# Softmax row sums in a two-head attention loop: matmuls over every probability tile against pair sums made on VectorE

## The reference, cut to what matters

```
x  : 8192 tokens x 4096, 32 heads, no mask, no causal cut
xn = layernorm(x)
q  = (xn @ Wq_c.T + bq_c) @ Wq_up.T + bq_up        # 192 per head: 128 + 64 rope
kv = xn @ Wkv_c.T + bkv_c                          # 512 latent + 64 rope, shared by the heads
k  = [kv_nope @ Wkv_up.T (128 per head), kv_rope]  ; v = 128 per head
attn = softmax(q @ k.T / sqrt(192))
out  = sum over heads of (attn @ v) @ Wo.T + bo    ; x = x + out
x    = x + layernorm(x) @ W.T + bias + LoRA terms
```

## Time and profile before

| | |
|---|---|
| runs before | 10136.65 and 9846.27 us, median 9991.46 us |
| the profiled execution | 9699.19 us |
| its span on the slowest core (core 5) | 9697.6 us |
| spans of the eight cores | 9638.9 to 9697.6 us |
| mean granted TensorE clock of core 5 | 0.839 |

### The profile page before, as it was taken

One profiled execution on the slowest core, in us unless ns is written; L12 is line 12 of the kernel. 1 busy time (PEld: TensorE's weight loads), 2 busy tenths in 40 slices (PEclk: granted clock), 3 DMA queues, 4 the chain that ended last, 5 costly groups with the idle time before them and its releaser, 6 DMA issues.

```text
span 9697.6 us, 97205 instructions; the slowest of 8 cores (9638.9 to 9697.6 us)
## 1 busy us (share of the span) xinstructions
PE 7616.9 (79%) x31944; PEld 2593.5 (27%) x31944; DVE 2710.9 (28%) x4102; ACT 3183.7 (33%) x5467; POOL 112.3 (1%) x232
## 2 busy tenths in 40 slices
PE   5464666666669889889899898898898898894777
PEld 2121323322222232332331331331322322311333
DVE  2012343344430330330331321321322312305211
ACT  1001222222205336336335345344354353351000
POOL 0100000000000000000000000000000000000000
PEclk8666666666679999999999999999999999995788
DMA  3634121121130000000000000000000000004444
GB/s 80 117 63 108 55 75 70 71 74 58 63 82 1 21 21 1 21 14 7 21 14 8 21 7 14 21 1 21 21 1 21 21 1 21 7 1 124 89 108 110
DMA packets 86382, 400.15 MB, mean 41 GB/s; under 512 B 9763, under 2 KB 22180, under 8 KB 67236
## 3 DMA queue, kind: packets, MB, share of 16 engines
q1 hardware_dynamic: 57574, 274.92, 8.1%
q0 software_dynamic: 28352, 119.03, 7.4%
HBM read 466.78 MB, written 46.14 MB: 53 GB/s over the span
## 4 chain that ended last, share of the span: by engine, by line
PE 73%; DVE 10%; issue 7%; DMA 7%; ACT 1%; DVEq 0%; SPq 0%; ACTq 0%; POOL 0%; POOLq 0%
PE ps L647 7%; PE ps L617 7%; PE ps L623 7%; PE ps L653 7%; PE ps L304 6%; PE ps L339 6%; PE ps L501 5%; PE ps L931 5%; PE ps L650 5%; PE ps L656 5%; PE ps L523 5%; PE ps L620 4%; DMA arena<-wqcT 3%; PE ps L548 3%; DVE st_sum L232 3%
## 5 line engine op out<-in xcount | busy, mean ns | idle before, releaser
L632 ACT ACTIVATE arena<-ps,sb_negc_col 128x512 bf16<-128x512 f32 x2048 | 1412.0, 689 | 3240.1 <-DVE sb_negc_col L605 1734.9
L634 ACT ACTIVATE arena<-ps,sb_negc_col 128x512 bf16<-128x512 f32 x2048 | 1397.0, 682 | 0.0
L304 PE MATMUL ps<-sb_id,arena 128*128 128x128 f32 x2048 | 775.8, 434 | 781.6 <-DVE arena L261 556.1
L666 DVE RECIPROCAL sb_recip<-ps 1x512 f32<-1x512 f32 x64 | 209.8, 3314 | 3956.3 <-PE ps L656 3956.3
L647 PE MATMUL ps<-arena 128*128 128x512 bf16 x2048 | 809.1, 395 | 35.2 <-DVE arena L691 35.2
L617 PE MATMUL ps<-arena 128*128 128x512 bf16 x2048 | 813.2, 397 | 27.8 <-ACT arena L634 27.8
L627 PE MATMUL ps<-arena 64*128 64x512 bf16 x2048 | 808.6, 395 | 0.0
L623 PE MATMUL ps<-arena 64*128 64x512 bf16 x2048 | 808.5, 395 | 0.0
L620 PE MATMUL ps<-arena 128*128 128x512 bf16 x2048 | 796.0, 389 | 0.0
L650 PE MATMUL ps<-arena 128*128 128x512 bf16 x2048 | 786.0, 384 | 0.0
L656 PE MATMUL ps<-arena,sb_onec 128*1 128x512 bf16 x2048 | 781.4, 382 | 0.0
(11 more groups left out here) (91 smaller groups left out, 5690.4 us busy)
## 6 DMA issues: line engine op xcount, KB each, us to landing
arena<-x_rot SPq DMA_DIRECT2D x72, 2048.0 KB, 10.0
arena<-wqcT POOLq DMA_DIRECT2D x128, 384.0 KB, 4.8
arena<-qcF_dram SPq DMA_DIRECT2D x32, 1536.0 KB, 6.4
arena<-wffn_til POOLq DMA_DIRECT2D x16, 2048.0 KB, 24.0
arena<-wqup_til POOLq DMA_DIRECT2D x16, 1152.0 KB, 11.8
x_dram<-arena SPq DMA_DIRECT2D x64, 256.0 KB, 4.1
arena<-x_dram SPq DMA_DIRECT2D x8, 2048.0 KB, 31.1
out_c<-arena SPq DMA_DIRECT2D x64, 256.0 KB, 2.4
```

Of the source, the lines that this page charges most:

```text
L304: tok_tp = em("t", lambda t, b=b, xb=a_xn[bi], dc=dc: t.transpose(bank(b)[:, 0:128], xb[:, dc * 128:dc * 128 + 128], sb_id[:, :]), sm_t)
L632: te0 = em("s", lambda s, b0=b0, kc=kc: s.activation(b_P[0][kc % 3], bank(b0), AF.Exp, bias=sb_negc_col[:, :]), sm_s)
L634: te1 = em("s", lambda s, b1=b1, kc=kc: s.activation(b_P[1][kc % 3], bank(b1), AF.Exp, bias=sb_negc_col[:, :]), sm_s)
```

## The change

The ones-matmuls no longer run on every probability tile. At each odd `kc`, VectorE adds the tile of step `kc - 1` and that of step `kc`, for each head (`tensor_tensor`, 128x512 bf16, all in SBUF), into a new tile `b_Ps[h][j]`, two per head, used in turn. `emit_pv` of an odd `kc` then runs the two ones-matmuls on the sums. `emit_pv` of an even `kc` has none. To make room, `b_bcast` and `b_otmp` go from two buffers each to one. New waits: an exp waits for the add that last read its tile (`p_read`), the ones-matmul for its add (`tps_tok`). The first PV matmul of a query block waits for banks 4 and 5 alone, the first ones-matmul for 6 and 7.

```diff
+        b_Ps = [[B.take(512, BF16) for _ in range(2)] for _ in range(2)]
...
                 wt("s", tok_sc)
+                wt("s", p_read[0][kc % 3])
+                wt("s", p_read[1][kc % 3])
                 te0 = em("s", lambda s, b0=b0, kc=kc: s.activation(
...
+                if kc % 2 == 1:
+                    for h, te in ((0, te0), (1, te1)):
+                        wt("v", te)
+                        wt("v", tps_free[h][(kc // 2) % 2])
+                        tok_add = em("v", lambda v, h=h, kc=kc: v.tensor_tensor(
+                            b_Ps[h][(kc // 2) % 2], b_P[h][(kc - 1) % 3],
+                            b_P[h][kc % 3], ALU.add), sm_v)
+                        tps_tok[h][(kc // 2) % 2] = tok_add
+                        p_read[h][(kc - 1) % 3] = tok_add
+                        p_read[h][kc % 3] = tok_add
...
-                em("t", lambda t, kc=kc: t.matmul(
-                    bank(6)[0:1, :], sb_onec[:, :], b_P[0][kc % 3],
-                    start=(kc == 0), stop=(kc == 63)))
-                return em("t", lambda t, kc=kc: t.matmul(
-                    bank(7)[0:1, :], sb_onec[:, :], b_P[1][kc % 3],
                     start=(kc == 0), stop=(kc == 63)),
                     sm_t if kc == 63 else None)
+                if kc % 2 == 1:
+                    j = (kc // 2) % 2
+                    if kc == 1:
+                        for ob in (6, 7):
+                            wt("t", bankfree[ob])
+                    for h in range(2):
+                        wt("t", tps_tok[h][j])
+                        tok = em("t", lambda t, kc=kc, h=h, j=j: t.matmul(
+                            bank(6 + h)[0:1, :], sb_onec[:, :], b_Ps[h][j],
+                            start=(kc == 1), stop=(kc == 63)),
+                            sm_t if kc == 63 else None)
+                        tps_free[h][j] = tok if kc == 63 else None
+                return tok
```

More of the change, by code:

```diff
@@ L431, in build_nc @@
         b_wkV = B.take(4 * 256, BF16).rearrange("p (c f) -> p c f", c=4)
-        b_bcast = [B.take(512, F32) for _ in range(2)]
-        b_otmp = [B.take(512, F32) for _ in range(2)]
+        b_bcast = B.take(512, F32)
+        b_otmp = B.take(512, F32)
+        b_Ps = [[B.take(512, BF16) for _ in range(2)] for _ in range(2)]
         b_osum = arena[:, OS_BASE:OS_BASE + 1024]
@@ L464, in build_nc @@
         texp = [(None, None)] * 3
+        tps_tok = [[None, None], [None, None]]
+        tps_free = [[None, None], [None, None]]
+        p_read = [[None] * 3, [None] * 3]
         tok_bc_prev = [None, None]
@@ L642, in emit_pv @@
                 if epi_banks_wait:
-                    for ob in (4, 5, 6, 7):
+                    for ob in (4, 5):
                         wt("t", bankfree[ob])
@@ L649, in emit_pv @@
                     start=(kc == 0), stop=(kc == 63)))
-                em("t", lambda t, kc=kc: t.matmul(
+                tok = em("t", lambda t, kc=kc: t.matmul(
                     bank(5), b_V[:, kc * 256 + 128:kc * 256 + 256], b_P[1][kc % 3],
-                    start=(kc == 0), stop=(kc == 63)))
-                em("t", lambda t, kc=kc: t.matmul(
-                    bank(6)[0:1, :], sb_onec[:, :], b_P[0][kc % 3],
-                    start=(kc == 0), stop=(kc == 63)))
-                return em("t", lambda t, kc=kc: t.matmul(
-                    bank(7)[0:1, :], sb_onec[:, :], b_P[1][kc % 3],
                     start=(kc == 0), stop=(kc == 63)),
                     sm_t if kc == 63 else None)
+                if kc % 2 == 1:
[11 more added lines that the diff above has]
+                return tok
             def emit_epi_v1(qb, tok_pv):
@@ L686, in flush_epi @@
                     wt("v", tok_bc)
-                    tcp = em("v", lambda v, bcb=bcb, h=h: v.tensor_copy(
-                        b_bcast[h], bank(bcb)), sm_v)
+                    tcp = em("v", lambda v, bcb=bcb: v.tensor_copy(
+                        b_bcast, bank(bcb)), sm_v)
                     bankfree[bcb] = tcp
@@ L691, in flush_epi @@
                     tmu = em("v", lambda v, h=h: v.tensor_tensor(
-                        b_otmp[h], bank(4 + h), b_bcast[h], ALU.mult), sm_v)
+                        b_otmp, bank(4 + h), b_bcast, ALU.mult), sm_v)
                     bankfree[4 + h] = tmu
@@ L695, in flush_epi @@
                     wt("v", tok_osum_chain[0])
-                    tok_osum_chain[0] = em("v", lambda v, qb=qb, h=h: v.tensor_tensor(
+                    tok_osum_chain[0] = em("v", lambda v, qb=qb: v.tensor_tensor(
                         b_osum[:, qb * 512:qb * 512 + 512],
-                        b_osum[:, qb * 512:qb * 512 + 512], b_otmp[h], ALU.add), sm_v)
+                        b_osum[:, qb * 512:qb * 512 + 512], b_otmp, ALU.add), sm_v)
             flush_fn[0] = flush_epi
```

## The result

The changed kernel takes 9445.01 us (median of 11 runs) against 10135.99 (median of 10) for the kernel before. In many executions the cores of a die are granted a lower clock for some of the time, whatever the kernel; the ratio leaves these out, and the profile of the changed kernel is read on the cores without it, 0 to 3. The ratio is 0.930, with a 95% interval of 0.920 to 0.939: faster, by 7%. It rests on few executions: the lowest were 9728 and 9788 us before, 9042, 9086 and 9093 us now. The sum had given a ratio of 0.948, 507 us less than the profiled execution.

A forecast was written before the change was run, and what follows sets the result against it. TensorE was taken to bound the kernel. 9699 - 532 + 3 + 22 gave 9192 us on the profiled execution, ratio 0.948, or 9469 on the median; the forecast was the middle, 9330, range 9130 to 9570.

The forecast's parts named there:

- The sum: Whole kernel: 9699 - 532 + 3 + 22 = 9192 us, 0.948 of the profiled execution.
- What bounds the kernel: Attention: TensorE sets the pace, busy throughout dense parts at clock 1.00, and ScalarE's exps wait for it.
- The signs: Profile after: right if double steps take 3.3 us; wrong if exps idle behind adds or the clock falls in dense stretches.
- Term 1: Attention steps: 1024 ones pairs removed at 0.52 us each, 532 us off TensorE.
- Term 2: Attention steps: 2048 VectorE adds hidden beside TensorE, except about 0.1 us at each of 32 block ends, 3 us.
- Term 3: Flush in the second query block: two adds ahead of the copy delay TensorE 1.4 us in 16 pairs, 22 us.
- Broken loads: Remaining ones pairs: a wait between the two matmuls stops the early weight load, 102 us more; chance 0.13.
- Loop over the tiles: Attention steps: exps, adds and next exps form a loop; at 1.0 us per add it costs 154 us; chance 0.04.
- Clock: Attention steps: denser full matmuls lower the clock; 1.2 GHz in 30% of double steps costs 774 us; chance 0.05.
- The estimate of 4.09: Attention double step in us, if a peak-current limit of 13/16 of the clock came with the change: 3.32 / 0.8125.

The follow-up runs named there:

- e4: The changed kernel without its adds and their waits, ones-matmuls reading only the odd step's tile: 3.213 us a double step, attention 5182 to 5185 us against 5196.
- e3: The kernel before plus the adds, the exps' waits for them and single flush buffers, sums never read: 3.840 us a double step, as in the kernel before.
- e1: The kernel before with 128 columns of ones as weights instead of one: 3.447 us a double step, 9311.5 us against 9706.9 for the run.
- e2: The kernel before with PV and ones-matmuls in turn instead of in pairs: 4.236 us a double step, spans 10217.7 to 10390.2 us.
- e5: The kernel before with 128 columns of ones and rope matmuls over all 128 rows: 3.453 us a double step, spans 9220.4 to 9287.9 us.
- e6: The changed kernel with 128 columns of ones as weights instead of one: 3.015 us a double step, spans 8815.1 to 8859.6 us.

## Why the prediction was right, and where it was off

- **What bounds the kernel: right.** TensorE's stream set the pace and still does. e4 shows that the removal is the whole gain, e3 that the adds don't touch the step.
- **The signs: one of the wrong ones came.** The exps have 589.5 us of idle time behind the adds (L649). It isn't the adds that they wait for: the first exp of a step starts 0.60 us behind the first rope matmul (L627) whether its wait is put down to an add (890 of them on core 1, median 0.602) or not (0.603). In e4, without adds and waits, it is 0.49. Of the right ones, two were missed in size. The double step is 3.21 and not 3.3, and at the flush L663 starts 0.14 us later and not 0.8 to 1.4.
- **Term 1: the mechanism right, the size off.** This is the term that was mis-sized. I priced a ones pair at 0.52 us, from PV to scores. What goes with it is 3.840 - 3.213 = 0.627 us, x 1024 = 642 instead of 532. The start-to-start distances were read correctly from the earlier trace rows, but the gap ahead of the ones pair was counted to PV, as if it would stay. It belongs to the change of shape, and two changes go with each pair. e1, e2 and e5 show this from three sides, with double steps of 3.447, 4.236 and 3.453 us against 3.46, 4.22 and 3.45 from the price of 0.095 per change.
- **Term 2, nearly nothing: right.** The exps start 0.11 us later, as allowed for. In the last step of each of the 32 blocks of core 1 the ones pair starts 0.31 us behind PV, the plain distance at a change of shape, so it doesn't wait for the add. What I had missed there is PV itself: it waits about 0.1 us for the later exp, 3.5 us in all. That the 3 us of the sum came out nearly so is luck, since they stood for another wait.
- **Term 3: the right place, too large.** I took 1.4 us x 16 = 22, by the row of the f32 add. The copy is 0.61 us later. The first PV matmul is 0.14 to 0.16 us later than in the kernel before, 3 us in all, and about 0.6 later than in e4, 10 us. I had taken VectorE for the one thing in the chain, and in the kernel before the spreading matmuls held it up too. The rule of the Trainium skill ("VectorE: DVE Perf Modes", the perf-mode tier table), from which I had estimated 424 ns for the bf16 add, was the better guide: the trace has 425. By it the term was 14.
- **The sum**, corrected: 9699 - 642 + 4 + 3 = 9064 instead of 9192 (4 for the last PV matmuls, 3 for the flush). These terms give -635. The attention has -637 to -641, and the whole spans of cores 0 to 3 have -631 to -650; what moved outside the attention, by up to 13 us, is not explained.
- **The ratio**, 0.930, lies below the 0.948 of the sum because of term 1: the corrected sum gives 0.935, within the interval.
- **The absolute time**, 9445, lies 115 above the 9330 of the forecast and within the range, which is partly luck. The median of the kernel before was 10136 with more runs and not 9991; 0.948 of that is 9609. The middle that I took, without a reason in the rows, made the forecast too low for such a median, term 1, too small by 110, made it too high, and the two partly cancelled. The range of 9130 to 9570 would have been too high for the lowest three executions, 9042 to 9093 us.
- **The rivals.** Broken loads: the two L677 are 0.215 apart, so the wait between them costs nothing; instead gaps vanished elsewhere. Its premise, that the first of each two matmuls pays for its weights, fell with e1. Loop over the tiles: excluded by e3, and an add takes 0.425 us where 0.93 was needed. Clock: 1.00 in the dense stretches of cores 0 to 3, but 0.81 in stretches of the attention on core 5, with a double step of 3.77 instead of 3.21. The kernel before has 0.81 as well, on core 5 from 156 to 200 us in stage A, and in other executions of it cores had a mean clock down to 0.768 instead of 0.84. So it isn't the change that brings it. The Trainium skill's peak-current limit ("TensorE: Matmul & The Clock Gate", Part 1) names 13/16 of the clock for a die with three cores in dense matmuls. The trace agrees on the size, 0.81, but not on the condition: all eight cores ran dense matmuls, and cores 0 to 3 never had 0.81. The estimate of 4.09 was above the 3.77 measured. What switches it on and off is not shown.

## What to carry to other kernels

Price a matmul that you mean to remove by the gaps on both of its sides, and look at the recorded rows x columns of its neighbours: where they differ, a gap goes with it. A narrow matmul (a column of ones) between full ones was made cheaper by making it as wide as they are (e1, e6), and matmuls of one shape did better standing together (e2). Adding tiles on an idle VectorE before they go through a ones-matmul pays as long as the adds don't stand ahead of something that TensorE waits for.

## What the runs showed of the hardware that I had not expected

- Between two matmuls of 512 columns with the same rows x columns of the array the distance was 0.216 us, and across a change, of rows or of columns, 0.31 to 0.32. With more columns of weights the kernel was faster: 128 instead of 1 took 383 us off the attention of core 1 (e1). Only three shapes were tried, 128*128, 128*1 and 64*128, and the two 128*1 matmuls of a step use the same column; other widths, and narrow matmuls with different weights, are not shown.
- Two matmuls on 64 rows each, side by side, cost 0.003 + 0.312 + 0.319 us with the changes around them, where two on all 128 rows cost 3 x 0.216 (e5), the distances from the matmul ahead to the one behind. That is no gain.
- At a granted clock of 0.81 a double step of the changed kernel took 3.77 us and not 3.213 / 0.8125 = 3.95 (core 5, 7205 to 7320 us).
- VectorE's reciprocal of 1x512 and of 128x512 both took 3.3 us.
